# Turning K by 32x32 blocks on VectorE, one score visit per batch, and last-token scores on GpSimd, in a three-part block of cross-attention, convolution and experts

## What is computed

```python
# 32 query heads, 8 key/value groups, head width 32; K and V are both the context
x = x + attention(layernorm(x), ctx, ctx, mask)      # softmax over 257 context tokens
x = x + s4_convolution(layernorm(x))                 # causal convolution over 1024, one kernel for all rows
x = x + experts(layernorm(x))                        # 64 experts of rank 8, top 16 by a router, softmax weights
```

## Time and profile before

| | before |
|---|---|
| median of 3 runs | 1413.99 us (1413.96 to 1414.87) |
| the profiled execution, its own time | 1416.3 us |
| its span, first to last instruction | 1414.5 us |
| PE busy | 1375.5 us, 97% |
| DVE busy | 1092.0 us, 77% |
| ACT busy | 1054.0 us, 75% |
| POOL busy | 282.5 us, 20% |
| DMA | 98.34 MB in 69458 packets |

### The profile page before, as it was taken

The page is one execution under the profiler, slowest core; times in us unless marked ns, Lnnn a source line. Parts: engine busy times, 40 slices in busy tenths (PEclk is TensorE's granted clock), DMA queues, the critical chain, the costliest instruction groups (busy, mean ns, idle before and its releaser), DMA issues.

```text
span 1414.5 us, 42025 instructions
## 1 busy us (share of the span) xinstructions
PE 1375.5 (97%) x14508; PEld 1175.3 (83%) x14508; DVE 1092.0 (77%) x3721; ACT 1054.0 (75%) x3137; POOL 282.5 (20%) x620
## 2 busy tenths in 40 slices
PE   4799999999999999999999999999999999999997
PEld 3678888888888888888888888888888888888886
DVE  7887777777777787777788777777887778877763
ACT  3787877777877777787777787777787777778750
POOL 1022221122222122222122222112222202222120
PEclk9999999999999999999999999999999999999998
DMA  4331212122212121221122221212121212222100
GB/s 164 90 102 59 81 55 67 64 81 58 81 55 81 51 81 60 78 75 61 53 78 66 73 81 55 78 54 81 58 81 60 76 51 81 66 73 66 59 18 30
DMA packets 69458, 98.34 MB, mean 70 GB/s; under 512 B 30697, under 2 KB 39538, under 8 KB 69250
## 3 DMA queue, kind: packets, MB, share of 16 engines
q1 hardware_dynamic: 69250, 95.66, 21.4%
HBM read 77.78 MB, written 16.78 MB: 67 GB/s over the span
## 4 chain that ended last, share of the span: by engine, by line
PE 95%; ACT 2%; DVE 2%; DMA 1%; issue 1%; SPq 0%; DVEq 0%; ACTq 0%
PE ps_p L496 31%; PE ps_p L601 16%; PE ps_p L586 16%; PE ps_p L614 13%; PE ps_s L528 10%; PE ps_p L547 9%; ACT pr L804 1%; DMA xq<-in_x 1%; ACT pts L754 0%; PE ps_p L507 0%; DMA ms<-in_mask 0%; DVE lns L1325 0%; DVE x L1164 0%; DVE ms L1286 0%; PE ps_p L478 0%
## 5 line engine op out<-in xcount | busy, mean ns | idle before, releaser
L804 ACT ACTIVATE pr<-ms,negmax 128x257 f32<-128x257 f32 x1024 | 513.9, 505 | 28.0 <-DVE negmax L1286 28.0
L1286 DVE CUSTOM_DVE_ANT_0 ms<-ps_s,neg_mask 128x257 f32<-128x257 f32 x1024 | 409.3, 418 | 113.5 <-PE ps_s L528 110.3
L754 ACT ACTIVATE pts<-ps_p 128x512 f32<-128x512 f32 x512 | 297.3, 595 | 116.7 <-PE ps_p L496 113.8
L496 PE MATMUL ps_p<-ident,pr 128*128 128x128 f32 x2048 | 302.9, 276 | 4.3 <-ACT pr L804 2.6
L496 PEld LDWEIGHTS ps_p<-ident,pr 128*128 128x128 f32 x2048 | 241.6, 142 | 29.3 <-issue 6.5
L804 ACT ACTIVATION_READ_ACCUMULATOR pr<-ms,negmax 128x1 f32 x1024 | 199.1, 194 | 0.0
L601 PE MATMUL ps_p<-wa_hi,ut_hi 128*128 128x288 f32 x512 | 177.1, 346 | 1.5 <-DVE ut_lo L1087 1.5
L528 PE MATMUL ps_s<-kt,qs 32*128 32x258 f32 x3072 | 163.0, 314 | 2.8 <-DVE negmax L1286 2.5
L528 PEld LDWEIGHTS ps_s<-kt,qs 32*128 32x128 f32 x3072 | 109.6, 185 | 52.6 <-issue 51.5
L601 PE MATMUL ps_p<-wa_lo,ut_hi 128*128 128x288 f32 x512 | 151.7, 296 | 0.0
L601 PE MATMUL ps_p<-wa_hi,ut_lo 128*128 128x288 f32 x512 | 151.4, 296 | 0.0
(11 more groups left out here) (142 smaller groups left out, 2501.1 us busy)
## 6 DMA issues: line engine op xcount, KB each, us to landing
cx<-in_ctx SPq DMA_DIRECT2D x128, 256.0 KB, 2.8
xq<-in_x SPq DMA_DIRECT2D x32, 512.0 KB, 4.0
xr<-in_x SPq DMA_DIRECT2D x32, 512.0 KB, 3.8
out_x<-tmp SPq DMA_DIRECT2D x32, 512.0 KB, 2.9
dn<-den SPq DMA_DIRECT2D x512, 2.0 KB, 1.8
vl<-in_ctx SPq DMA_DIRECT2D x128, 32.0 KB, 3.4
x<-in_L_ffn_A_w SPq DMA_DIRECT2D x2, 512.0 KB, 5.6
xr<-in_L_ffn_B_w SPq DMA_DIRECT2D x2, 512.0 KB, 3.6
```

Of the source, the lines that this page charges most:

```text
L496: mm = pe.transpose(into[:, j * P:(j + 1) * P], source, ident[:, :])
L754: return act.activation(out, in_, ACT.Copy, scale=scale)
L804: act.activation(pr[:, b % 2, g, 0:CTX_LEN], ms[:, n % MS, 0:CTX_LEN], ACT.Exp, bias=negmax[:, n % MS:n % MS + 1], scale=-1.0, accum_out=d ...
L1286: dve.tensor_tensor_reduce(ms[:, n % MS, 0:CTX_LEN], ps_s[:, n % GPH, 0:CTX_LEN], neg_mask[:, :], 1.0, MAX_FLOAT, ALU.add, ALU.min, negmax ...
```

## The change

- K is loaded a second time. `load_keys` (SP) brings a batch's 256 tokens in four DMAs with pieces of 256 bytes into `kx`, so that the blocks of 32 tokens by 32 features lie in the partitions that they must end in; DVE's `k_turn` transposes all 32x32 blocks of a 128x512 tile in one instruction into `kr`. `k_chunk` is gone from PE. `k_high` copies `kr` to `kt`, and `k_low` moves from DVE to POOL.
- K for tile `it + 1` is prepared during iteration `it` for all four batches. `kx` has two buffers, `kr` one: `load_keys` of batch b waits for the turn of batch b - 2, `k_turn` for POOL's `k_low` of the batch before.
- `scores(it, b)` makes both halves of a batch at one visit: 24 matmuls, 256 columns each, both halves of the columns of the four banks. The maxima of a whole batch must be done before it.
- The last token's scores are made on POOL: `last_product` multiplies the normalised queries with the last context row, `last_sum` halves the 32 columns five times, `last_mask` adds the mask; `store_last` and `turn_last` (SP) bring them through DRAM into the layout of the scores (one store, four loads per tile). `maximum` starts from them and takes 256 columns; the first maximum of a batch waits for `last_shift` of the batch before, which reads `negmax`; `last_shift` (POOL) and `last_exp` (ACT) make their exponentials. `last_chunk`, `last_high`, `last_low`, `last_column`, `last_probs` are gone. `normalisers` gets one addition more.
- `first_residual` moves from DVE to POOL.
- The halves of a batch are now the even and the odd groups, so `x1`, `tmp` and `xr` are read in strided halves there. The context load now puts tokens 128 apart on a partition (1 KB pieces), and is made later.
- The order lists of all engines, and the banks, are laid out anew. Among them: `attend` for batches 2 and 3 stands in two places instead of one, and the experts' second part is made two iterations after the tile's attention.

```diff
-SW = CTX_LEN + 1
+SW = 2 * P
...
-        ktl = sb("ktl", [P, 2, 2, HALVES, BPT], F32R)
-        cxl = sb("cxl", [BPT, CTX_DIM])
+        kx = sb("kx", [P, 2, GROUPS, HALVES, HEAD_DIM])
+        kr = sb("kr", [P, HALVES, 2 * P])
...
-                             .rearrange("o (p j) f -> (o p) j f", j=TBLK)).then_inc(cx_loaded[b], 16)
+                             .rearrange("o (j p) f -> (o p) j f", j=TBLK)).then_inc(cx_loaded[b], 16)
+
+            def load_keys(tile, b):
+
+                if at(tile, BPT, b - 1) > 0:
+                    sp.wait_ge(kr_done, at(tile, BPT, b - 1))
+                turned = context[tile * BPT + b:tile * BPT + b + 1, 0:2 * P, :].rearrange(
+                    "o (c t) (q e) -> (o t) c q e", t=HEAD_DIM, q=GPH)
+                for quad in range(GPH):
+                    sp.dma_start(kx[HEAD_DIM * quad:HEAD_DIM * (quad + 1), b % 2, :, :, :].rearrange("p c h d -> p c (h d)"),
+                                 turned[:, :, quad, :]).then_inc(kx_loaded[b], 16)
 
...
+            def store_last(tile):
+                sp.wait_ge(lm_done, at(tile, 1, 1))
+                if at(tile, 64, 0) > 0:
+                    sp.wait_ge(last_loaded, at(tile, 64, 0))
+                sp.dma_start(turn.rearrange("b s n -> (b s) n"), lasts[:].rearrange("p r g -> p (r g)")).then_inc(last_stored, 16)
+
+            def turn_last(tile):
+                sp.wait_ge(last_stored, at(tile, 16, 16))
+                if at(tile, STEPS, 1 - STEPS) > 0:
+                    sp.wait_ge(ms_done, at(tile, STEPS, 1 - STEPS))
+                if at(tile, BPT, -BPT) > 0:
+                    sp.wait_ge(ld_done, at(tile, BPT, -BPT))
+                for r in range(REP):
+                    sp.dma_start(last[SEQ * r:SEQ * (r + 1), tile % 2, :, :],
+                                 turn[:, :, GROUPS * r:GROUPS * (r + 1)].rearrange("b s g -> s b g")).then_inc(last_loaded, 16)
 
...
             def iteration(it, odd):
+                store_last(it)
+                turn_last(it)
+                load_context(it, 0)
+                if on(it - 1):
+                    move_den(it - 1, 2)
+                    load_context(it - 1, 2)
                 if on(it - 3):
                     store(it - 3)
                 if on(it - 1):
                     move_den(it - 1, 3)
+                if on(it + 1):
+                    load_keys(it + 1, 0)
                 load_context(it, 3)
+                if on(it + 1):
+                    load_last(it + 1)
+                load_residual(it)
+                move_den(it, 0)
+                load_context(it, 1)
                 if on(it + 2):
                     load_x(it + 2)
+                if on(it + 1):
+                    load_keys(it + 1, 1)
                 move_den(it, 1)
                 if on(it + 1):
+                    load_keys(it + 1, 2)
+                    load_keys(it + 1, 3)
...
-            def last_chunk(tile):
-                pe.wait_ge(cxl_loaded, at(tile, 16, 16))
-                into = take("last", 0, tile, ll_done, at(tile, 1, 1))
+            def scores(it, b):
+                pe.wait_ge(kl_done, at(it, BPT, b + 1))
+                if b == 0:
+                    pe.wait_ge(ql_done, at(it, 2, 2))
+                pe.wait_ge(ms_done, at(it, STEPS, GROUPS * b))
                 for h in range(HALVES):
-                    mm = pe.transpose(into[:, h * BPT:(h + 1) * BPT], cxl[:, h * P:(h + 1) * P],
-                                      ident[0:BPT, 0:BPT])
-                mm.then_inc(lt_done, 1)
-
+                    for j, (q_part, k_part) in enumerate(((0, 0), (0, 1), (1, 0))):
+                        for quad in range(GPH):
+                            rs = slice(HEAD_DIM * quad, HEAD_DIM * (quad + 1))
+                            mm = pe.matmul(ps_s[:, quad, h * SW:(h + 1) * SW], qs[rs, it % 2, q_part, b, h, :, :].rearrange("p r s -> p (r s)"),
+                                           kt[rs, b, k_part, h, :], start=(j == 0), stop=(j == 2), skip_group_check=True)
+                            if j == 2 and h == HALVES - 1:
+                                mm.then_inc(s_done, 1)
 
...
                 scores(it, 0)
+                if on(it - 1):
+                    pair_chunk(it - 1, 12)
+                if on(it - 2):
+                    experts(it - 2, 1, 0, 8)
                 if on(it - 1):
                     pair_chunk(it - 1, 13)
                     pair_chunk(it - 1, 14)
+                    attend(it - 1, 4); attend(it - 1, 5)
                     pair_chunk(it - 1, 15)
+                scores(it, 1)
+                pair_chunk(it, 0)
+                if on(it - 1):
                     attend(it - 1, 6); attend(it - 1, 7)
                 if on(it - 2):
+                    experts(it - 2, 0, 0, 5)
                 if on(it - 1):
                     out_chunk(it - 1, 0)
                 pair_chunk(it, 1)
+                if on(it - 2):
+                    experts(it - 2, 0, 5, 8)
+                pair_chunk(it, 2)
                 if on(it - 1):
                     out_chunk(it - 1, 1)
                 if on(it - 2):
+                    gated_chunk(it - 2)
+                pair_chunk(it, 3)
+                scores(it, 2)
+                pair_chunk(it, 4)
+                if on(it - 2):
                     expand(it - 2, 0, 0, 2)
+                pair_chunk(it, 5)
                 if on(it - 2):
                     expand(it - 2, 0, 2, 4)
+                    expand(it - 2, 1, 0, 4)
+                pair_chunk(it, 6)
+                if on(it - 1):
+                    u_chunk(it - 1, 0)
+                if on(it + 1):
+                    q_chunk(it + 1, 0)
+                if on(it - 1):
+                    u_chunk(it - 1, 1)
                 attend(it, 0); attend(it, 1)
...
+            def last_exp(it, b):
+                act.wait_ge(ld_done, at(it, BPT, b + 1))
+                if at(it, 64, 0) > 0:
+                    act.wait_ge(den_moved[b], at(it, 64, 0))
+                act.activation(den[:, b, GROUPS:2 * GROUPS], lasd[:, b % 2, :], ACT.Exp, scale=-1.0).then_inc(le_done, 1)
...
+            def k_low(tile, b):
+                pool.wait_ge(kh_done, at(tile, BPT, b + 1))
+                pool.tensor_tensor(kt[:, b, 1, :, 0:2 * P], kr[:, :, :], kt[:, b, 0, :, 0:2 * P].bitcast(F32),
+                                   ALU.subtract).then_inc(kl_done, 1)
+
+            def last_product(tile, h):
+                if h == 0:
+                    pool.wait_ge(vl_loaded, at(tile, 64, 64))
+                pool.wait_ge(xq_used, at(tile, 2, h + 1))
+                if at(tile, 1, 0) > 0:
+                    pool.wait_ge(lm_done, at(tile, 1, 0))
+                v = vl[:, tile % 2, :].rearrange("p (q h d) -> p h q d", q=GPH, h=HALVES)[:, h, :, :].unsqueeze(1).broadcast_to([P, REP, GPH, HEAD_DIM])
+                pool.tensor_tensor(lastp[:, h, :, :, :], qn[:, h, :, :].rearrange("p r (q d) -> p r q d", q=GPH), v, ALU.mult).then_inc(lp_done, 1)
+
+            def last_sum(tile, k0, k1):
+                for k in range(k0, k1):
+                    if k == 0:
+                        pool.wait_ge(lp_done, at(tile, 2, 2))
+                    else:
+                        pool.wait_ge(ls_done, at(tile, LAST_STEPS, k))
+                    w = HEAD_DIM >> (k + 1)
+                    near, far = (lastp[:, :, :, :, a:a + w].rearrange("p h r q d -> p (h r q) d") for a in (0, w))
+                    pool.tensor_tensor(near, near, far, ALU.add).then_inc(ls_done, 1)
+
+            def last_mask(tile):
+                pool.wait_ge(ls_done, at(tile, LAST_STEPS, LAST_STEPS))
+                if at(tile, 16, 0) > 0:
+                    pool.wait_ge(last_stored, at(tile, 16, 0))
+                if tile == 0:
+                    pool.wait_ge(su_mask, 1)
+                pool.tensor_scalar(lasts[:].rearrange("p r (h q) -> p h r q", h=HALVES), lastp[:, :, :, :, 0],
+                                   neg_mask[:, 2 * P:CTX_LEN], None, ALU.add).then_inc(lm_done, 1)
+
+            def last_shift(it, b):
+                pool.wait_ge(ms_done, at(it, STEPS, GROUPS * (b + 1)))
+                if at(it, BPT, b - 1) > 0:
+                    pool.wait_ge(le_done, at(it, BPT, b - 1))
+                pool.tensor_tensor(lasd[:, b % 2, :], last[:, it % 2, b, :], negmax[:, :], ALU.subtract).then_inc(ld_done, 1)
 
...
+            def first_residual(tile, h):
+                pool.wait_ge(oa_done, at(tile, 2, h + 1))
+                pool.wait_ge(tm_done, at(tile, 4, 2 * h + 2))
+                pool.tensor_tensor(half(x1, h), half(x1, h), half(tmp, h), ALU.add).then_inc(x1_done, 1)
 
...
+                last_mask(it)
+                k_low(it, 2)
+                if on(it - 1):
+                    last_shift(it - 1, 3)
+                if on(it - 2):
+                    row_scale(2, it - 2)
                 if on(it + 1):
                     row_scale(0, it + 1)
+                k_low(it, 3)
+                last_shift(it, 0)
```

(64 more changed lines are left out.)

## The result

The changed kernel takes 1323.19 us (median of 4 runs, 1322.49 to 1324.92), the kernel before in the same session 1414.43 us (1413.96 to 1415.39). The ratio is 0.9356, 95% interval 0.934 to 0.9372: 91 us faster, 10 us better than the 1333 forecast and inside the range. The profiled execution took 1324.9 us, its span is 1323.1.

What follows compares the result with a forecast made beforehand. TensorE's list was taken as the bound: -3.41 us per iteration over 29 iterations (-98.9), -2.9 tile 31, +15 stalls, +4 start, +1.5 drain turn 1416.3 into 1335, 1333 as median; 8 in 10: 1306 to 1374.

Steps and rivals of the forecast that it cites:

- The K chunks: PE, loop: `k_chunk`, four transposes done four times per iteration, leaves the list: -1.74 us per iteration.
- the entry into a score visit: PE, scores: entering and leaving the row-grouped form costs 0.39 us; 4 visits of 24 for 8 of 12 save 1.56.
- the extra attention visit: PE: `attend` for batches 2 and 3 no longer stands together, one visit more: +0.29 us per iteration.
- `last_chunk`: PE, once per iteration: its work leaves the list, -0.40 us.
- The stalls: New hand-over waits in the loop: 0.5 us per iteration, +15 us in all; bounds 0 and 1.7 (+49).
- the drain: After the loop: `first_residual` runs on POOL for 1.3 us where DVE took 0.7, +1.5 us.
- the chain: K issues, store and loads of last-token scores before maximum 0: 7.7 us, landing 0.9 us early to 1.1 late.
- My second rival place: First maximum of each batch waits for POOL's `last_shift`; before maximum 24, over 2 us to spare unless sums cost 6.7.
- the block transposes: DVE: four 32x32 block transposes of 128x512 per iteration, taken at 0.6 us each, between 0.535 and 3.35.
- a bound of 2 us: DVE, shared port: at most six meetings of 1.3 us with POOL, 2 us of DVE per iteration.
- The start: Before the loop: first maximum later by up to 10 us, half covered by DVE's set-up work: +4 us.
- tile 31: PE behind the loop: this tile still saves three `k_chunk` and four entries, -2.9 us.

Runs made afterwards that it cites:

- the constant: Changed kernel with every maximum starting its minimum from a constant instead of the last-token score in SBUF: 1320.42 us, ratio 0.9336 to the kernel before.
- short GpSimd operations: Changed kernel with GpSimd's last_share, residual, first_residual and last_sum handling only a small part of their columns: 1318.26 us, ratio 0.9311 to the kernel before.
- Two stores: Changed kernel with SyncE storing the last-token scores twice, the second after the first has landed: 1323.89 us, ratio 0.937 to the kernel before.
- five: Changed kernel with the last-token scores stored five times, each after the one before has landed: 1441.96 us, ratio 1.0208 to the kernel before.
- the last experiment: Changed kernel with the K split moved back from GpSimd to VectorE from tile 3 on: 1333.77 us, ratio 0.9427 to the kernel before.

## Why the prediction was right, and where it was off

- **The bound.** That PE's list sets the period, and that its microseconds come back 29 times, held in three ways: PE busy throughout, +1.71 for 1.74 us of added transposes, and no gain in the loop when DVE was relieved of 1.8 us (the constant) or of 1.2 (short GpSimd operations).
- **PE's terms.** The K chunks were 1.74 by forecast and 1.71 by experiment, the entry into a score visit 0.39 and 0.39, the extra attention visit 0.29 and 0.17. The sum 3.41 met 3.39. That it met it so closely is in part luck: the measured parts, with `last_chunk` as forecast, would make 3.51. The price of an entry came from taking the known neighbours off the stretch around a visit; the bare slots would have given half. The earlier trace rows showed that a lengthened group pays its entry once.
- **The stalls, the term that was mis-sized.** Booked: 0.5 us per iteration, 15 us. Measured: about 0.04 us, 1 us in all. With the 4 us that the drain took more than booked, the two make the 10 us between 1333 and 1323. It came from a misreading of the code: `load_keys(tile, b)` waits for `kr_done` at b - 1, which is the turn of batch b - 2. So `load_keys(it + 1, 3)` goes after `k_turn(it + 1, 1)`, behind maximum 22, not after `k_turn(it + 1, 2)`, behind maximum 26. That is one turn and four maxima earlier, 5.6 us in the rows above (602.82 against 608.43). The prediction's 7.7 us for the chain, counted from the end of the right turn (603.53), give 611.2, where the loads landed at 611.9; counted from the wrong one they give 616.8, just behind maximum 0's 616.65. So the lengths in the chain were right and its starting point was wrong, and the margin is 4.8 us. Two stores showed no cost, five the cost that this margin gives. My second rival place, `last_shift` behind POOL's sums, showed nothing either: the first maxima of a batch wait for PE.
- **DVE.** 30.7 forecast, 33.9 measured. The maxima are 1.7 us of the difference (60 ns each for the starting value, less a little for 256 columns), which I had taken as unchanged; the block transposes 0.4 (0.706 against 0.6, the wrong choice between two kinds of rows, see the last section); GpSimd on the shared port about 1.5 (the router's steps and `row_norm`), of which the prediction spoke with a bound of 2 us, but left it out of the sum. Together these estimates are 0.4 more than the difference. It changed nothing because PE had the longer list; at 38.5 us it would have.
- **POOL.** 22.3 for 21. K splits 1.40 (1.345 taken), products 1.30 (1.08 taken), the five sums 3.05 (3.1 taken), mask and shifts 1.5 (1.0 taken).
- **The ends.** The start: +3.9 for +4, from the two profiled executions (110.7 and 114.6 us until tile 2 begins). This hit is luck: executions of the edits that leave the start as it is begin tile 2 at 111.8 to 113.7 us. The drain: +2.6 us in the same two executions, with nearly the same granted clock there (0.95 and 0.96), where -2.9 for tile 31 and +1.5 had been booked. The PE groups behind the loop, before and after, show why:

```profile
L601 PE MATMUL ps_p<-wa_hi,ut_hi 128*128 128x288 f32 x39 | 13.0, 332 | 1.5 <-DVE ut_lo L1087 1.5
```

```profile
L633 PE MATMUL ps_p<-wa_hi,ut_hi 128*128 128x288 f32 x48 | 15.5, 322 | 1.4 <-DVE ut_lo L1137 1.4
```

  Nine products more of each of three kinds, 27 x 0.133 = 3.6 us, and four transposes more: the experts' second part now comes an iteration later, so more of it is left behind the loop. With the -1.4 booked for the drain they make +2.6. The section on the change names the move; the sum had no term for it.

Added up: -97.8 in the loop, +3.9 before it, +2.6 behind it make -91.3, and 1416.3 - 91.3 = 1325.0 is the profiled 1324.9.

The best version found is the changed kernel with its maxima started from a constant, 1320.42 us; its interval of the ratio overlaps with that of the changed kernel, so no gain is shown.

## What to carry to other kernels

Where one engine is busy for the whole loop, count what leaves its list, and price entering and leaving a special form by the change that one more visit makes to its neighbours, not by the visit's own slot. Before booking a stall, write each semaphore's index down with numbers for one iteration, for an off-by-one there is worth microseconds; and price a piece of work that is moved not by its length alone but by the round trip that it covered where it stood. Before giving an edit a difference of a few microseconds, compare the two executions stretch by stretch, with the granted clock of each.

## What the hardware showed beyond the forecast

- A 32x32 block transpose of 128x512 fp32 on DVE takes 0.706 us, a third more than the one-source operation of that size (0.535) and near the two-source ones (0.69). The rows below show why 0.535 was the wrong neighbour. The one-source operation goes from 0.535 to 0.813 us when its columns double to 1024, 0.54 ns a column. A two-source operation goes from 0.191 us for 32 columns to 0.687 for 512 (the K split on DVE in the last experiment), 1.03 ns a column and 0.16 us before the first (an estimate from these two rows). By the rule of the Trainium skill (Vector Engine (DVE) Microarchitecture Reference, section 3.8), one element per cycle and lane, the prediction had expected the low end; but that rule is a rate, without a fixed part, and one measured size neither confirms nor refutes it.

```profile
L1360 DVE TENSOR_SCALAR un<-x,lns 128x1024 f32<-128x1024 f32 x29 | 23.6, 813 | 1.7
```

```profile
L1420 DVE TENSOR_TENSOR dn<-dn 128x32 f32<-128x32 f32 x29 | 5.5, 191 | 1.0
```

- A starting value read from SBUF adds 60 ns to DVE's 0.411 us add-and-minimum of 256 columns.
- A change of form on PE shows as a gap between starts on both sides of a tiled visit: 605.28 to 605.50 before the score visit above, where one product to the next takes 0.12. Behind a visit, 0.20 us pass from its last matmul to the next product (median of the loop). From `attend` to scores it is one such gap and not two: `attend` takes the same 1.01 us before scores (846.24 to 847.25) as before transposes.
- DVE's operations with two SBUF sources are stretched by long GpSimd operations even when they handle one column: 0.153 against 0.407 us on average. It works the other way too: GpSimd's K split took 1.75 us instead of 1.29 where `row_norm` was running when it started.
- The clock in the start is lower, 0.92 against 0.98 for the first 106 and 110 us, with PE busy for 64.2 us against 80.8. The edits' executions show 0.94 to 0.97 there, with PE busy for 61 to 67 us. Whether PE's thinner work is the reason was not tried.
